# Moving the low parts of the weights of a row recurrence behind the first normalised row, with constants multiplied meanwhile

## The reference

```python
x: (4, 1024, 48, 48) float32          # image, channel, row, column
xn = group_norm(x, groups=32)          # mean and variance of 32 channels x 48 x 48, per image
Wm = W[:, :, 4, 0]; bb = b[None, :, None]          # 1024 x 1024
def step(carry, row): new = relu(einsum('oc,ncw->now', Wm, carry) + bb) + row; return new, new
down = rows 0..47 of xn, each new row from the row above it
up   = the same, in reverse, over the rows of down
return x + up
```

## Time and profile before

| | |
|---|---|
| median of 3 runs | 1700.72 us |
| the profiled execution's own time | 1700.67 us |
| its span, first to last instruction | 1698.9 us |
| TensorE busy | 1568.6 us, 92% |
| ScalarE, VectorE, GpSimd busy | 76%, 69%, 53% |
| granted clock of TensorE, mean | 0.998 |

### The profile page before, as it was taken

How to read it: one execution, slowest core, us unless ns; L and a number is a source line. 1 busy time by engine, 2 the same in 40 slices (tenths; PEclk the granted TensorE clock), 3 DMA queues, 4 the chain that set the end, 5 groups by cost and what they waited for, 6 DMA issues and landing times.

```text
span 1698.9 us, 23271 instructions
## 1 busy us (share of the span) xinstructions
PE 1568.6 (92%) x6796; PEld 1292.4 (76%) x6796; DVE 1169.7 (69%) x3357; ACT 1294.1 (76%) x3969; POOL 897.4 (53%) x1001
## 2 busy tenths in 40 slices
PE   0019999999999999999999999999999999999997
PEld 0007888888888888888888888888888888888886
DVE  7897666666666666666666666666666666666665
ACT  0027888888888888888888888888888888888886
POOL 0037666666666666666665454454454454445443
PEclk9999999999999999999999999999999999999999
DMA  9982323223232322222001434343343434344211
GB/s 350 373 265 75 112 77 110 92 95 111 77 112 75 112 87 100 102 85 75 1 1 38 167 113 167 124 156 138 142 157 123 168 114 165 130 150 149 75 57 56
DMA packets 61647, 207.02 MB, mean 122 GB/s; under 512 B 4176, under 2 KB 32848, under 8 KB 61520
## 3 DMA queue, kind: packets, MB, share of 16 engines
q1 hardware_dynamic: 61376, 205.54, 33.9%
q10 hardware_dynamic: 144, 0.00, 0.0%
HBM read 136.32 MB, written 69.21 MB: 121 GB/s over the span
## 4 chain that ended last, share of the span: by engine, by line
PE 91%; DMA 4%; DVE 3%; SPq 1%; ACT 0%; issue 0%; POOLq 0%; POOL 0%; ACTq 0%; DVEq 0%
PE bank L524 30%; PE bank L519 30%; PE bank L522 30%; DMA x_ring<-x_rows 2%; DMA d_ring<-x_rows 2%; DVE turn L379 1%; SPq L223 1%; DVE moments L390 0%; DVE d_ring L424 0%; DVE d_ring L427 0%; DVE w_lo L445 0%; DVE st_lo L431 0%; DVE turn L456 0%; ACT turn L353 0%; DVE d_ring L471 0%
## 5 line engine op out<-in xcount | busy, mean ns | idle before, releaser
L519 PE MATMUL bank<-w_hi,st_hi 128*128 128x512 f32 (+1 forms) x2264 | 888.4, 392 | 7.4 <-ACT st_hi L320 6.8
L524 PE MATMUL bank<-w_hi,st_lo 128*128 128x512 f32 (+1 forms) x2264 | 888.3, 392 | 0.9 <-DVE st_lo L431 0.6
L522 PE MATMUL bank<-w_lo,st_hi 128*128 128x512 f32 (+1 forms) x2264 | 887.5, 392 | 0.0
L344 ACT ACTIVATE turn<-turn 32x128 f32<-32x128 f32 x2256 | 701.4, 311 | 106.0 <-DVE turn L451 82.5
L293 POOL TENSOR_TENSOR st_lo<-d_ring,st_hi 128x256 fp32r<-128x256 f32 x558 | 404.2, 746 | 663.4 <-ACT st_hi L359 663.4
L456 DVE STREAM_TRANSPOSE turn<-bank 32x128 f32<-32x128 f32 x2256 | 708.7, 314 | 35.7
L519 PEld LDWEIGHTS bank<-w_hi,st_hi 128*128 128x128 f32 (+1 forms) x2264 | 430.7, 190 | 98.7 <-ACT st_hi L320 7.0
L524 PEld LDWEIGHTS bank<-w_hi,st_lo 128*128 128x128 f32 (+1 forms) x2264 | 430.5, 190 | 94.2 <-DVE st_lo L431 2.0
L522 PEld LDWEIGHTS bank<-w_lo,st_hi 128*128 128x128 f32 (+1 forms) x2264 | 430.7, 190 | 91.1 <-issue 1.0
L353 ACT ACTIVATE turn<-turn,bias_sb 128x128 f32<-128x128 f32 (+1 forms) x1132 | 364.3, 393 | 37.8 <-DVE turn L456 0.8
L359 ACT ACTIVATE st_hi<-d_ring 128x256 fp32r<-128x256 f32 x558 | 215.8, 438 | 137.8 <-DVE d_ring L471 137.8
(11 more groups left out here) (28 smaller groups left out, 81.1 us busy)
## 6 DMA issues: line engine op xcount, KB each, us to landing
x_ring<-x_rows SPq DMA_DIRECT2D x88, 768.0 KB, 7.0
out_rows<-x_ring SPq DMA_DIRECT2D x48, 768.0 KB, 4.1
down_rows<-d_ring SPq DMA_DIRECT2D x40, 768.0 KB, 4.1
d_ring<-down_rows SPq DMA_DIRECT2D x40, 768.0 KB, 5.6
d_ring<-x_rows SPq DMA_DIRECT2D x12, 1536.0 KB, 16.2
x_ring<-x_rows SPq DMA_DIRECT2D x8, 1536.0 KB, 16.4
d_ring<-w_t SPq DMA_DIRECT2D x16, 256.0 KB, 7.7
bias_sb<-bias ACTq DMA_DIRECT2D x1, 4.0 KB, 2.5
```

The lines of the kernel that those rows point to most:

```text
L344: final = act.activation(target(j, q, u), source(blocks, q, u), ACT.Copy)
L519: pe.matmul(out, stationary(st_hi, j, k), w_cols(w_hi, o, k), start=(n == 0), stop=False)
L522: pe.matmul(out, stationary(st_hi, j, k), w_cols(w_lo, o, k), start=False, stop=False)
L524: last = pe.matmul(out, stationary(st_lo, j, k), w_cols(w_hi, o, k), start=False, stop=final)
```

## The change

The low parts of the weights are no longer begun when the first rounded tile is there. GpSimd waits until both halves of chunk 0 of row 0 are normalised (`first_row` at 2), and then makes tiles 0 to 3 and 8 to 11. VectorE makes 4 to 7 behind the two splits of chunk 0 and 12 to 15 behind the split of chunk 1; the normalisation of chunk 2 comes after those. ScalarE rounds the tiles 8 to 15 in one run ahead of the split of chunk 1. Jobs 0 and 1 run all 8 high-high matmuls, all 8 low-high ones, and then the 8 high-low ones, which are those that read `w_lo`. Behind the second small matmul TensorE runs 8 float32 matmuls of the constant matrix with itself, into a bank that is overwritten later. The last group of x comes in 5 loads: three of two channel tiles, two of one; statistics and moments follow these pieces.

```diff
+LAST_PIECES = ((0, 2), (2, 4), (4, 6), (6, 7), (7, 8))
-W_POOL = 13
+W_POOL = (0, 1, 2, 3, 8, 9, 10, 11)
+W_DVE = (4, 5, 6, 7, 12, 13, 14, 15)
+WARM = 8
 # SyncE
-            for k in range(K):
-                if k % TC == 0:
-                    sp.wait_ge(stats_done, (LAST - 2) * STAT_CHUNKS + k // TC + 1)
-                cols = slice(k * COLS, (k + 1) * COLS)
+            for n, (k0, k1) in enumerate(LAST_PIECES):
+                sp.wait_ge(stats_done, (LAST - 2) * STAT_CHUNKS + k0 // TC + 1)
+                cols = slice(k0 * COLS, k1 * COLS)
                 sp.dma_start(x_ring[:, :, cols], x_rows[0:RING, :, cols].rearrange("h p e -> p h e")
-                             ).then_inc(last_loaded[k], 16)
+                             ).then_inc(last_loaded[n], 16)
 # GpSimd
-            for t in range(W_POOL):
+            pool.wait_ge(first_row, 2)
+            for t in W_POOL:
 # ScalarE
-            for t in range(K, K + 3):
+            for t in range(K, W_TILES):
                 w_round(t)
             first_split(2, 1, 0, K)
-            for t in range(K + 3, W_TILES):
-                w_round(t)
             first_split(3, 2, 0, K)
 # VectorE
+            for n, (k0, k1) in enumerate(LAST_PIECES):
+                dve.wait_ge(last_loaded[n], 16)
+                channel_stats(x_ring, LAST, range(k0, k1)).then_inc(stats_done, 1)
+                if n >= 1:
+                    channel_moments(n - 1)
+            channel_moments(len(LAST_PIECES) - 1)
...
             first_split(1, 0, 0, KB)
-            first_normalise(2, 1, 0, K)
-            first_normalise(3, 2, 0, K)
-            first_split(2, 1, 0, K)
-            for t in range(W_POOL, W_TILES):
+            def w_rest(t):
...
+            for t in W_DVE[:KB]:
+                w_rest(t)
+            first_normalise(2, 1, 0, K)
+            first_split(2, 1, 0, K)
+            for t in W_DVE[KB:]:
+                w_rest(t)
+            first_normalise(3, 2, 0, K)
             first_split(3, 2, 0, K)
 # TensorE
+            for n in range(WARM):
+                pe.matmul(bank[5][:, 0:P], group_avg[:, :], group_avg[:, :], start=True, stop=True)
...
+            for j in range(2):
+                for n in range(K):
+                    product_hh(j, n)
+                for n in range(K):
+                    product_lh(j, n, False)
+                for n in range(K):
+                    last = product_hl(j, n, n == K - 1)
+                last.then_inc(acc_ready, 1)
+            for j in range(2, JOBS):
...
+                    product_hh(j, n)
+                    product_hl(j, n, False)
+                    last = product_lh(j, n, n == K - 1)
```

More of the change, by code:

```diff
@@ L174, in build @@
         stat_loaded = [[sem(f"stat_loaded{a}_{c}") for c in range(STAT_CHUNKS)] for a in range(2)]
-        last_loaded = [sem(f"last_loaded{k}") for k in range(K)]
+        last_loaded = [sem(f"last_loaded{n}") for n in range(len(LAST_PIECES))]
         bias_loaded = sem("bias_loaded")
@@ L385, in _, with channel_moments @@
                     channel_stats((d_ring, x_ring)[g % 2], g, range(c * TC, (c + 1) * TC)).then_inc(stats_done, 1)
-            def channel_moments(k):
-                dve.wait_ge(stats_done, LAST * STAT_CHUNKS + k + 1)
-                for i in range(k * NI, (k + 1) * NI):
+            def channel_moments(n):
+                k0, k1 = LAST_PIECES[n]
+                dve.wait_ge(stats_done, LAST * STAT_CHUNKS + n + 1)
+                for i in range(k0 * NI, k1 * NI):
                     final = dve.bn_aggr(moments[:, i, :], bn[:, i, :])
                 final.then_inc(moments_ready, 1)
[L393 to L398, removed]
+            for n, (k0, k1) in enumerate(LAST_PIECES):
[4 more added lines that the diff above has]
+            channel_moments(len(LAST_PIECES) - 1)
             dve.wait_ge(mean_summed, 1)
-            dve.wait_ge(moments_ready, K)
+            dve.wait_ge(moments_ready, len(LAST_PIECES))
             dve.tensor_tensor(delta[:, :], moments[:, :, 0], bank[6][:, 0:K * NI], ALU.subtract).then_inc(bn_step, 1)
@@ L482, in _ @@
             pe.wait_ge(const_ready, 1)
-            pe.wait_ge(moments_ready, K)
+            pe.wait_ge(moments_ready, len(LAST_PIECES))
             pe.matmul(bank[6][:, 0:K * NI], group_avg[:, :], moments[:, :, 0],
@@ L491, in wait_w @@
                 t = w_order(o, k)
-                if rest is None or t < W_POOL:
+                if rest is None:
                     pe.wait_ge(ready, t + 1)
+                elif t in W_POOL:
+                    pe.wait_ge(ready, W_POOL.index(t) + 1)
                 else:
-                    pe.wait_ge(rest, t - W_POOL + 1)
+                    pe.wait_ge(rest, W_DVE.index(t) + 1)
             def wait_split(ready, first, j, n):
@@ L506, in wait_split, with product_hh, product_hl, product_lh @@
                         pe.wait_ge(ready, second_done(j - CHUNKS))
-            for j in range(JOBS):
-                o = j % 2
-                out = bank[j % BANKS][0:used(j), :]
+            for n in range(WARM):
+                pe.matmul(bank[5][:, 0:P], group_avg[:, :], group_avg[:, :], start=True, stop=True)
+            def product_hh(j, n):
+                o, k = j % 2, KB * blocks_of(j)[n // KB] + n % KB
+                wait_split(hi_ready, first_hi, j, n)
+                if j < 2:
+                    wait_w(w_hi_ready, None, o, k)
+                return pe.matmul(bank[j % BANKS][0:used(j), :], stationary(st_hi, j, k), w_cols(w_hi, o, k),
+                                 start=(n == 0), stop=False)
+            def product_hl(j, n, final):
+                o, k = j % 2, KB * blocks_of(j)[n // KB] + n % KB
+                if j < 2:
+                    wait_w(w_lo_ready, w_lo_rest_ready, o, k)
+                return pe.matmul(bank[j % BANKS][0:used(j), :], stationary(st_hi, j, k), w_cols(w_lo, o, k),
+                                 start=False, stop=final)
+            def product_lh(j, n, final):
+                o, k = j % 2, KB * blocks_of(j)[n // KB] + n % KB
+                wait_split(lo_ready, first_lo, j, n)
+                return pe.matmul(bank[j % BANKS][0:used(j), :], stationary(st_lo, j, k), w_cols(w_hi, o, k),
+                                 start=False, stop=final)
+            for j in range(2):
[7 more added lines that the diff above has]
+            for j in range(2, JOBS):
                 if j >= BANKS:
```

## The result

The changed kernel takes 1704.84 us (median of 12 runs, 1704.57 to 1705.15), the one before 1700.72 in its 12 runs: 4.1 us longer, a ratio of 1.0024 with an interval of 1.0015 to 1.0033. The profiled execution took 1704.57 us, with a span of 1702.8.

What follows compares the result with a forecast made beforehand. VectorE's queue was taken to bound job 3's start: the profiled 1700.67 us plus 4.2 on VectorE plus 2.0 for the clock made 1706.9, given as 1706.8 us. The range was 1703.6 to 1709.0 us.

Steps and rivals of the forecast that it cites:

- The sum on VectorE: VectorE's queue up to the turn of job 0: all costs and savings together +4.2 us, bounds +3.0 and +5.5.
- What bounds the kernel: Ahead of job 3: VectorE's queue sets its start; an earlier job 0 buys nothing unless that queue gets shorter.
- Loads, +0.97: Last x loads: VectorE waits 0.52 and 0.45 us for the first two larger pieces, +0.97 us, bounds 0 and 2.2.
- The gain, -2.0 and -3.0: VectorE with GpSimd held back: lines 416 and 419 save 2.0 us, chunk 0's first three operations 3.0 us.
- The payback: VectorE after the hold: chunk 0's splits +1.9, tiles +7.3, chunk 1's normalisation +1.1, chunk 2's -2.0, later splits -0.1 us.
- What was costed at nothing: TensorE before job 3: waits behind VectorE's tiles and 5 us of constants stay hidden if job 1 ends by 144.6.
- The clock, +2.0: Job 3's start at 150.25: TensorE idles 3.4 us before it, the clock falls, +2.0 us, between 0 and 3.5.
- The rival of a clock that stays up: Ahead of job 3: the gap is shorter or starts later, so the clock stays up: 1704.9 us, chance 0.22.
- The turning point of the rival without turns: VectorE and GpSimd not excluding each other: 1694.2 us, chance 0.05; tiles under 0.9 us beside GpSimd would decide it.

Runs made afterwards that it cites:

- `job3_whole`: The changed kernel with job 3 made to wait at its first matmul for the chunk of the row above as completed by job 1: 1709.19 us.
- `all_on_vector`: The changed kernel with all 16 tiles of the low weights on VectorE and none on GpSimd: 1702.11 us.

## Why the prediction was right, and where it was not

The direction was right and the measured time lies in the range, between the forecast of 1706.8 and its lower end. The sum on VectorE was right in its terms; the 2.0 us for the clock were not, and that the time is in the range all the same is owed to a range wide enough for a kernel without them. By its steps:

- **What bounds the kernel.** Right: the end follows VectorE's queue. The turn of job 0 moved by 3.96 us and the profiled execution by 3.90.
- **Loads, +0.97.** Measured 1.1 in the trace (first small matmul at 113.71 instead of 112.62) and 1.1 by taking them back. The transfers did move faster: 372 GB/s from 92 to 94 us and 367 from 96 to 98, where the single loads had 328, and VectorE waited 0.44 us per piece. The Trainium skill ("DMA: Bandwidth & Descriptors", section Specifications) had spoken for no gain in rate, by which the wait would have been 1.1 us per piece; the trace doesn't agree with it.
- **The gain, -2.0 and -3.0.** Measured -2.1 and -3.0: `gn_rstd` ends at 117.13 instead of 118.11, and chunk 0's four operations take 1.7 us instead of 4.7.
- **The payback.** Splits of chunk 0 +2.2 (1.9 forecast), tiles +7.1 (7.3), chunk 1's normalisation +1.1 (1.1), chunk 2's -2.0 (-2.0), the two later splits -0.4 (-0.1). With the loads and the gain the whole sum is 3.96 where 4.2 was forecast.
- **What was costed at nothing.** Right for the constants, which took 3.6 us (5 taken, 1.7 to 7.4 as bounds): jobs 0 to 2 waited for tiles and chunks on VectorE with or without them.
- **The clock, +2.0. This step failed.** It rests on job 3's start at 150.25 behind an idle TensorE. The row at 146.05 is job 3's thirteenth matmul, not its first: the wait in the code is on `first_done` (what job j-3 made) at the first channel tile and on `second_done` (what job j-2 made) at the fifth, and I had put only the second into the argument and into the section on the kernel before. TensorE had three and a half jobs to do before 146.05, not three. Counting matmuls would have told: in the kernel before 60 matmuls start from 131.10 to 145.06, behind job 0's last: two jobs and a half. The 12 matmuls fill 2.8 of the 3.4 us, so only 0.57 us of idle time were there and the granted clock stayed at 1.00 around 150. The rival of a clock that stays up, at 1704.9, had the time right: it allowed for a shorter gap, but not for this reason. `job3_whole` shows that the price was sound: with the gap the clock falls and costs 1.55 us, though later than the step had it.
- **The turning point of the rival without turns** (tiles of 0.9 us) doesn't come out of its own sum: 7 x 0.7 is 4.9, where 4.2 were to be undone, 0.6 a tile, so about 1.0 us. Nothing hangs on it, as tiles took 1.7.

The trace had also been read right on the two engines taking turns, which was one rival's point: an operation of 512 columns takes 0.6 to 0.7 us alone and, where it meets one of GpSimd in full, 1.6 to 1.8, in the kernel before and in the changed one. The Trainium skill ("SBUF — State Buffer", section SBUF: two separate sides) says that the port pair of the two is locked for a whole instruction and the other engine waits; the traces agree, as an operation of VectorE that meets one of GpSimd takes about 1.0 us longer. The prediction had the payback behind the hold in its sum. What it did not ask is what the hold is worth with the new share of the tiles: it gives 1.0 us and not 5.0, and moves the meetings of the two engines instead of removing them.

That the change as a whole loses is thus settled by subtraction: 1.1 us for the loads, 3.2 for the hold with the tiles it pushes back. Not tried was the hold on the kernel before alone, so how the hold does with the old share of tiles is open.

## What to carry to other kernels

Before work is divided between two engines, read from the trace what one operation takes alone and beside the other. Here VectorE alone made a tile in 0.61 us, and both together two in 1.67 where VectorE alone needs 1.22. So the helper made the pair slower, and the gain came from letting it run only beside operations that it doesn't meet (the statistics). Starting an engine earlier, or warming it, is worth something only if it is what the next step waits for. Before a gap is priced, count the instructions that fill it, from the waits in the code.

## What the runs showed of the hardware that was not expected

- In `job3_whole` the granted clock fell some 1.3 us **after** TensorE had started again at 150.25, behind an idle time of 3.3 us in which it stayed at 1.00. A gap can be paid for in the work behind it, where no idle time is seen. In the changed kernel it fell earlier in a gap: at about 129, behind a stretch from 124.8 on in which TensorE did five matmuls, and some 3.7 us before job 1 started.
- The constants, 16 float32 passes of 128 columns, took 3.4 to 3.8 us, 0.21 to 0.23 each: half of the 0.43 us of a 512-column matmul of the reduced type near the start of the kernel before. Behind them those matmuls stand 0.24 apart from the first on (0.33 in `all_on_vector`).
- The rate of loads from HBM rose with the length of their runs: 328 GB/s with runs of 768 bytes (768 KB a load), 373 with 1536 bytes (1.5 MB), and 386 from 112 to 116 us in the kernel before for W's tiles, runs of 2048 bytes in loads of only 256 KB. So a larger load alone is not what raises it.
- GpSimd's tiles took 1.24 us beside `bn_stats` and `bn_aggr`, and those took no longer for it: 1.53 us for 8 `bn_aggr`, as in the changed kernel with GpSimd idle (1.54). Of VectorE's operations seen here those with two inputs in SBUF are the ones that meet it, down to one of 32 columns: 1.20 us against 0.19.
